# A third tree fetched by row, Silu in place in PSUM, Nyquist sums in two products, and a new order on all engines

## The reference

```python
x = x + attn(layernorm(x));  x = x + ffn(layernorm(x))
# attn: q, k, v = unit_projection(h @ W.T + b)   each frequency divided by its size
#       s = cumsum over the sequence of bind(k, v) = ifft(fft(k) * fft(v))
#       out = unbind(s, q) = ifft(fft(s) * conj(fft(q)))
# ffn:  logits = h @ W_in.T + b_in               8 trees of 255 nodes, depth 7
#       walk each tree from its root, right where the logit is > 0: 8 nodes on the path
#       out = (silu(logits) * on_path) @ W_out.T
```

## Time and profile before

| | |
|---|---|
| median of 3 runs | 1975.06 us (1973.09 to 1975.19) |
| span of the profiled execution, first to last instruction | 1972.4 us |
| the profiled execution's own time | not listed apart; the span is 2.66 us under the median |
| busy: PE, DVE, ACT, POOL | 1883.7, 1579.8, 1118.8, 917.0 us |
| one step in the middle of the loop | 58.56 us |
| start of the first `logits` | 111.50 us |

### The profile page before, as it was taken

How to read it: one execution, slowest core, us unless ns; L and a number is a source line. 1 busy time by engine, 2 the same in 40 slices (tenths; PEclk the granted TensorE clock), 3 DMA queues, 4 the chain that set the end, 5 groups by cost and what they waited for, 6 DMA issues and landing times.

```text
span 1972.4 us, 40210 instructions
## 1 busy us (share of the span) xinstructions
PE 1883.7 (96%) x14680; PEld 1410.5 (72%) x14680; DVE 1579.8 (80%) x2874; ACT 1118.8 (57%) x2151; POOL 917.0 (46%) x736
## 2 busy tenths in 40 slices
PE   8599999999999999999999999999999999999978
PEld 6468777777777777877777877777777777786755
DVE  4887888887888888788888788888788888878783
ACT  5566555566555556555556655556655555655543
POOL 1254444555444555444555444455544455534450
PEclk9799999999999999999999999999999999999998
DMA  8032133222223222223222213222222322222212
GB/s 278 11 86 87 54 96 95 65 85 85 64 85 96 75 80 80 82 67 96 83 77 85 85 53 96 94 66 85 85 64 85 96 75 79 81 71 79 86 54 65
DMA packets 181784, 163.18 MB, mean 83 GB/s; under 512 B 140160, under 2 KB 140800, under 8 KB 181760
## 3 DMA queue, kind: packets, MB, share of 16 engines
q1 hardware_dynamic: 163328, 95.48, 16.2%
q0 software_dynamic: 18432, 67.38, 10.2%
HBM read 95.72 MB, written 16.78 MB: 57 GB/s over the span
## 4 chain that ended last, share of the span: by engine, by line
PE 74%; DVE 10%; ACT 6%; issue 3%; DMA 0%; ACTq 0%; SPq 0%; DVEq 0%
PE bank_l L531 26%; PE bank_p L481 24%; PE bank_l L591 17%; DVE arena L1220 9%; ACT arena L796 3%; ACT arena L705 2%; PE bank_i L481 2%; PE bank_l L541 2%; ACT arena L806 1%; PE bank_i L552 1%; PE bank_i L562 0%; PE bank_i L559 0%; PE bank_i L560 0%; PE bank_i L561 0%; DVE sp_z L1178 0%
## 5 line engine op out<-in xcount | busy, mean ns | idle before, releaser
L591 PE MATMUL bank_l<-wout_mem,arena 128*128 128x512 f16 x2688 | 606.7, 379 | 38.6 <-DVE arena L1220 38.6
L531 PE MATMUL bank_l<-arena,win_mem 128*128 128x256 f16 x5376 | 626.0, 273 | 14.0 <-DMA arena<-xn_pair 14.0
L531 PEld LDWEIGHTS bank_l<-arena,win_mem 128*128 128x128 f16 x5376 | 527.5, 99 | 75.7 <-DMA arena<-xn_pair 14.2
L591 PEld LDWEIGHTS bank_l<-wout_mem,arena 128*128 128x128 f16 x2688 | 255.5, 98 | 365.8 <-DVE arena L1220 84.3
L481 PE MATMUL bank_p<-arena,wf_hi 128*128 128x256 f16 x3072 | 505.9, 273 | 2.7 <-ACT arena L742 2.7
L986 POOL TENSOR_TENSOR arena<-arena 128x512 f32<-128x512 f32 x96 | 121.9, 1270 | 658.5 <-ACT arena L751 658.5
L481 PE MATMUL bank_p<-arena,wf_lo 128*128 128x256 f16 x1536 | 419.1, 273 | 0.0
L1220 DVE SCALAR_TENSOR_TENSOR arena<-arena,s_act 128x512 f16<-128x512 f32 (+1 forms) x256 | 341.5, 1344 | 28.9 <-ACT arena L806 25.6
L481 PEld LDWEIGHTS bank_p<-arena,wf_hi 128*128 128x128 f16 x3072 | 299.7, 98 | 37.6 <-ACT arena L742 3.0
L796 ACT ACTIVATE arena<-bank_l,bias_in,s_logit 128x256 f32<-128x256 f32 x448 | 229.6, 556 | 142.0 <-PE bank_l L541 141.6
L1213 DVE TENSOR_SCALAR dec<-bank_l,thr,off 128x256 bf16<-128x256 f32 x256 | 135.8, 541 | 121.2 <-PE bank_l L531 120.0
(11 more groups left out here) (178 smaller groups left out, 2607.2 us busy)
## 6 DMA issues: line engine op xcount, KB each, us to landing
arena<-in_x SPq DMA_DIRECT2D x32, 512.0 KB, 3.4
arena<-arena SPq DMA_DIRECT2D x32, 512.0 KB, 2.9
out<-arena SPq DMA_DIRECT2D x64, 256.0 KB, 2.1
wout_mem<-in_w_in_t SPq DMA_DIRECT2D x1, 3584.0 KB, 14.6
arena<-in_w_out_t SPq DMA_DIRECT2D x1, 3584.0 KB, 14.6
arena<-xn_pair SPq DMA_TRANSPOSE x128, 2.7
arena<-in_leaf_rows,leaf_row POOLq DMA_INDIRECT x128, 5.6
win_mem<-in_wq SPq DMA_DIRECT2D x1, 1024.0 KB, 8.5
```

The lines of the kernel that those rows point to most:

```text
L531: mm = pe.matmul(bank_l[t % 4][:, c * T:(c + 1) * T], a[:, k, w:w + P], x2t[:, :, b, k, :], start=(c == 0 and k == 0 and m == 0), stop=((t ...
L591: mm = pe.matmul(bank_l[j][:, :], a[:, m, tok], w[:, m, :], start=(m == 0 and a is a_hi and w is wout_hi), stop=(m == DENSE - 1 and a is a ...
```

## The change

- `GATHERED` is (0, 1, 2) for (0, 1): 13 columns for 14, six indirect fetches in a step for four.
- `silu` writes over the logits in PSUM, and `act_high` and `act_low` read them there; the SBUF ring `acts` goes. A bank is free only when `act_low` has read it, so `logits` and `down` wait for `a_lo_ready` where they waited for `act_ready`.
- `nyquist_sums` makes its three columns in two matmuls for five; `nyquist_bind` prepares `sp_kv` with three small instructions for one.
- The order of the groups is K, V, Q for Q, K, V, in the loads, the prologue and every step.
- `unbind` waits after each product until it has been written.
- The prologue: thirty dummy matmuls first, K's weights loaded first, `project(1, ...)` ahead of the first `transform_back`, and all four `wout_high`/`wout_low` in step 0.
- `decide` has four buffers (`HELD`), and every engine's list in `step` is in a new order.

```diff
-GATHERED = (0, 1)
+GATHERED = (0, 1, 2)
-HELD = 3
+HELD = 4
-Q, K, V, G_IN, G_OUT = range(5)
+K, V, Q, G_IN, G_OUT = range(5)
+WARM = 30
...
-        acts = take(HELD * 2 * T).rearrange("p (r t) -> p r t", r=HELD)
...
                 if c == 0 and t >= 4:
 
-                    pe.wait_ge(act_ready, TREES * i + t - 3)
+                    pe.wait_ge(a_lo_ready, TREES * i + t - 3)
...
-                pe.matmul(sp_sums[:, 0:1], upper, sp_kv[:, 0:1], start=True, stop=True)
-                pe.matmul(sp_sums[:, 1:2], upper, sp_kv[:, 1:2], start=True, stop=False)
-                pe.matmul(sp_sums[:, 1:2], full, sp_kv[:, 0:1], start=False, stop=True)
-                pe.matmul(sp_sums[:, 2:3], full, sp_kv[:, 0:1], start=True, stop=False)
-                pe.matmul(sp_sums[:, 2:3], full, sp_kv[:, 1:2], start=False, stop=True).then_inc(sp_sums_full, 1)
+                pe.matmul(sp_sums[:, 0:3], upper, sp_kv[:, 0:3], start=True, stop=False)
+                pe.matmul(sp_sums[:, 0:3], full, sp_kv[:, 2:5], start=False, stop=True).then_inc(sp_sums_full, 1)
...
                 act.wait_ge(count_full, TREES * i + t + 1)
-                if t >= HELD:
-                    act.wait_ge(a_lo_ready, TREES * i + t + 1 - HELD)
-                elif not isinstance(i, int) or i:
-                    act.wait_ge(a_lo_ready, TREES * i)
                 for c in [c for c in range(2) if (t, c) in COLUMN]:
-                    ins = act.activation(acts[:, t % HELD, c * T:(c + 1) * T], bank_l[t % 4][:, c * T:(c + 1) * T],
+                    ins = act.activation(bank_l[t % 4][:, c * T:(c + 1) * T], bank_l[t % 4][:, c * T:(c + 1) * T],
                                          ACT.Silu, bias=bias_in[:, c, t:t + 1], scale=s_logit[:, 0:1])
...
                 dve.scalar_tensor_tensor(out=a_lo[:, m, :],
-                                         in0=acts[:, t % HELD, 0:wide * T].rearrange("p (c t) -> p c t", c=wide),
+                                         in0=bank_l[t % 4][:, 0:wide * T].rearrange("p (c t) -> p c t", c=wide),
                                          scalar=s_act[:, 0:1], in1=a_hi[:, m, :], op0=ALU.mult,
                                          op1=ALU.subtract).then_inc(a_lo_ready, 1)
...
-                pool.tensor_tensor(prod[:, 0], sr, qr, ALU.mult)
-                pool.tensor_tensor(prod[:, 1], si, qi, ALU.mult)
-                pool.tensor_tensor(prod[:, 2], si, qr, ALU.mult)
+                pool.tensor_tensor(prod[:, 0], sr, qr, ALU.mult).then_inc(z_prod, 1)
+                pool.wait_ge(z_prod, 4 * n + 1)
+                pool.tensor_tensor(prod[:, 1], si, qi, ALU.mult).then_inc(z_prod, 1)
+                pool.wait_ge(z_prod, 4 * n + 2)
+                pool.tensor_tensor(prod[:, 2], si, qr, ALU.mult).then_inc(z_prod, 1)
+                pool.wait_ge(z_prod, 4 * n + 3)
                 pool.tensor_tensor(prod[:, 3], sr, qi, ALU.mult).then_inc(z_prod, 1)
...
```

More of the change, by code:

```diff
@@ L266, in build @@
         sp_hat_ready = sem("sp_hat_ready")
+        sp_bound = sem("sp_bound")
         sp_kv_ready = sem("sp_kv_ready")
@@ L864, in first @@
                     fold_high(m)
-                for c in range(PIECES):
-                    win_rows(c)
-                    fold_high(KT + c)
+                projection_rows(Q)
+                for m in range(KT):
+                    fold_high(KT + m)
                 act.wait_ge(consts_done, 1)
+                evac_re(0, K)
+                evac_im(0, K)
+                square(0, K)
+                fold_high(2 * KT)
+                root(0, K)
+                win_rows(0)
+                win_rows(1)
+                evac_re(0, V)
+                evac_im(0, V)
+                square(0, V)
+                fold_high(2 * KT + 1)
+                root(0, V)
+                fold_high(2 * KT + 2)
+                win_rows(2)
+                fold_high(2 * KT + 3)
+                win_rows(3)
+                std(1, mv1, rs1, ln1_mv, ln1_std)
                 evac_re(0, Q)
@@ L1074, in step @@
                     add_eps(n, K)
+                    sum_squares(n, Q)
+                    add_eps(n, Q)
+                    bind(n)
+                for g in range(LEAVES):
+                    fetch(i, g)
+                if attn:
                     q_unit(n)
-                    bind(n)
-                fetch(i, 1)
-                fetch(i, 0)
-                if attn:
                     unbind(n)
```

364 lines of the change are left out of this document (191 added, 173 removed).

## The result

The changed kernel takes 1950.63 us, the median of four runs (1946.7 to 1958.03), against 1974.3 us for the kernel before beside it: a ratio of 0.9891, 95% interval 0.9879 to 0.9904. It is faster, by 1.1%; the forecast was 1895 us and its range 1842 to 1937. Both missed. The profiled execution of after is the slowest of the four, 1958.03 us with a span of 1956.2.

What follows compares the result with a forecast made beforehand. PE's own work bounds the kernel, with a little of DVE. Step: 58.56 - 3.25 - 1.17 + 1.70 + 0.35 = 56.2 us; 30 steps save 71.1, ends 6.2 and 2.6: span 1892.5, plus 2.7, 1895 us; range 1842 to 1937.

Steps and rivals of the forecast that it cites:

- PE's work: Matmuls of one step: fewer logits and `down` columns and Nyquist matmuls save 3.25 us, 57.39 becomes 54.14 us.
- The old wait: PE's wait for `act_low` at `down`: goes with `act_low` from PSUM, 1.17 us less per step.
- the bank's longer hold: PSUM banks of the logits, held until `act_low` has read them: costs nothing.
- The new wait: PE at the first logits, as `evac_im` stands ahead of `high` on ACT: 1.70 us per step.
- The 0.35 us of allowance: End of the step on DVE, dots meeting POOL's unbinding: 0.35 us per step added for what spills over.
- DVE's end: Rival: ten of twelve dots and additions meet POOL, late results bound the step at 57.6 us; 1938 us, chance 0.18.
- The prologue: Before the first logits: transform some 6 us earlier, logits at 102 for 111.50, -9.5 us; bounds 0 and -15.7.
- a hole: PE's idle time from 60 to 80 us: the 15.7 us of `project(1)` move into it.
- Step 0: Four `wout_low` between DVE's decisions make them late, +6.6 us; first full `project` still 6.2 us earlier than 154.87.
- ACT and POOL: Two more table loads, 2.57 us of ACT, cost nothing; POOL ends z at T+52.8, ahead of PE's T+54.6.
- Last block: Block without projection: one column less of logits and of `down`, 2.6 us less.

Runs made afterwards that it cites:

- e10: Changed kernel without the waits between POOL's unbinding products, and with the Nyquist sums in five one-column matmuls again; 1975.31 us.
- b1: Kernel before with only `silu`, `act_high` and `act_low` in PSUM and tree 1's two instructions moved ahead; 2139.75 us, ratio 1.0849.
- e3b: Changed kernel with 18 throwaway matmuls on PE between projections and first logits of steps 1 to 30; 1920.55 us, ratio to before 0.9727.
- e13: The kernel of e3b once more, on another chip beside e14 and e15; 1913.22 us.
- e15: The changed kernel, unchanged, run again as control beside e13 and e14; 1950.83 us.
- e1: Changed kernel with ACT's `evac_im` of the second group behind `high` of the second layer norm, as in the kernel before; 1934.28 us.
- e5: Changed kernel with another order of PE, ACT and DVE in the prologue alone, `project(0, Q)` ahead of W_in's peak among others; 1946.81 us.
- e14: Changed kernel with e3b's 18 throwaway matmuls and e5's prologue order together, run beside e13 and e15; 1905.76 us, ratio to before 0.9677.
- e7: Changed kernel with e5's prologue and, on ACT, `std` and `high` of xn2 ahead of `square(K)` and `evac_im(V)`; 1977.68 us.
- e9: The kernel of e7 with DVE's `decide` of tree 0 ahead of `kv_denominator` and the first inverse; 2039.92 us.
- b4: Kernel before with only `GATHERED = (0, 1, 2)`, its dots, additions and fetches added where the others stand; 2227.61 us, ratio 1.1292.
- e6: Changed kernel with `GATHERED = (0, 1)`, the third tree dense again and the rest of the change kept; 2189.54 us.
- e12: Changed kernel with 9 throwaway matmuls, for e3b's 18, before the first logits; 1943.59 us.
- e8: Changed kernel with e5's prologue, e1's edit and DVE's `decide(i, 0)` ahead of `kv_denominator` and the first inverse; 1977.39 us.

## Why the prediction was wrong

It was right that the kernel gets faster, and in the mechanisms that it wrote down for a step. Two steps of it failed: it left what the granted clock does after the new wait out of the sum, and it had the prologue's path wrong. By its own steps, in the profiled run (span 1956.2 for 1892.5 forecast, 63.7 us too much):

- **PE's work**: 54.14 us forecast, 53.73 measured at full clock. Right to 0.4 us, whose place no run shows; e10 gives the sums their 0.66 us.
- **The old wait**: goes, as forecast. But the bank's longer hold costs nothing only by the new order; b1 shows 4.9 us of waits a step without it. The walk that said so was right, for this order. (It names nine columns of `down(i,0)` ahead of T+44.6; its own list and its 44.6 have eleven.)
- **The new wait**: 1.70 us forecast, 2.12 measured. The place and the releaser were right to 0.02 us (`high` at T+11.83); the way from `high` to the logits was short by 0.45 us. It rested on the last block of before, where the second transpose lands in 2.75 us. In after it takes 3.11 us in the step shown and 3.15 in the last block, so it isn't the place in the step that makes it longer; why it is longer in the changed kernel stays open.

```profile
1924.92 2.75 DMA arena<-xn_pair
1912.38 3.15 DMA arena<-xn_pair
```

- **The 0.35 us of allowance**: nothing spilled over. Work 0.41 less, wait 0.42 more and this 0.35 less make a step at full clock 0.3 us shorter (55.88) than the 56.2 forecast. Over 30 steps the forecast was 10 us too high here. DVE's end, a rival, doesn't bound.
- **Not in the sum at all: the granted clock.** "Step: 58.56 - 3.25 - 1.17 + 1.70 + 0.35 = 56.2 us" counts a microsecond of waiting as a microsecond. Here 2.1 us of idleness cost 2.1 and then another 1.67 in 23 of 30 steps, 38 us in the run. That is the larger of the two failed steps, shown by e3b and by e13 against e15. The prediction read a clock of 0.66 in the prologue and 1.00 in the step, and didn't ask what a new gap would do to it.
- **The prologue**: "the transform some 6 us earlier than its end near 92.0". It ends at 118.0 for 86, 32 us late, and the way from there to the logits takes 18.7 us for 16: 102 became 136.66. The step looked at DVE's list alone (`win_low`). In PE's new list the peaks of W_in stand ahead of `project(0, Q)` and those of W_out ahead of the inverse transform; in ACT's, four `win_high` and four `wout_rows`, 13.1 us from 82.47 to 95.56, stand ahead of the evacuations for which `project(1)` waits. How much of the 34.7 us each part is worth, the runs show only in part. The clock's fall at 20 us is 9, in this run (by after against e1). The orders that e5 undoes are 6.5. The other 19 us are open: in e14, which has neither, `project(1)` still holds PE from 73.93 to 91.63 (below), the transform starts at 96.4, behind three `win_low` on DVE, and the logits at 121.3. The 15.7 us that were to go into a hole stand ahead of the transform, but no run moves them back.

```profile
73.93 17.70 PE bank_p L484 x144
```

- **Step 0**: from the first logits to the first full `project` the walk gives 46.7 us (148.7 less 102), and 46.75 were measured. That is in part luck: PE waits 4.42 us for decisions, not 6.6, and the half clock behind the two waits fills the rest (4.47 us for the first 24 logits, 4.83 for the 24 behind the late decision, against 2.79). So all of the 34.7 us by which the first full `project` is late (183.41 for 148.7) were lost by the first logits.
- **ACT and POOL**: nothing waits for the two table loads or for z at the inverse transform. Right.
- **Last block**: -2.4 us for -2.6.

Together 38 - 10 + 34.7 = 63 of the 63.7 us; the profiled run is also 7 us above the median of its kernel, which is why the medians are only 56 us apart. That size fits the 9 us of the fall at 20 us; no trace shows whether the other three runs had it. With those 9 us the clock is 47 of the 63.7. The range was too narrow: its upper end was the price of DVE's end, and no case had a slower clock or a slower start, although the prologue's bounds were known to be those of a guess.

## What to carry to other kernels

Price a new wait of TensorE twice: its length, and what follows it at half the clock; where the wait can't go, matmuls that compute nothing may be worth more than another order (37.6 us here; of four other orders of ACT and DVE, e1's gained some 15 us and e7's to e9's lost). When a change reorders every engine, follow each engine's list through the prologue and not only the one that was late before. A part that does no harm in the full change may cost 8 or 13% alone (b1, b4), so its worth can't be read from an experiment with one part. And compare two prologues by traces in which the clock fell at the same places.

## What the runs showed of the hardware

- **The clock.** At the first logits, PE's gap of 2.1 to 2.2 us is followed by 0.50 for 3.4 us, with PE busy, in 22 of 29 steps of after, 20 of e15, 24 of e10, and in none of e6, which has the same gap there but a longer one of 3.08 us later in the step, with the fall at that one. Gaps of 0.94 and 0.65 us with 2.8 us of work between (e1), of 1.17 us (e12) and of 0.20 us (e13) brought no fall in any step. The length of a gap alone doesn't decide: 1.97 us for a decision (e8) had a fall in 2 of 29 steps, 1.2 and 1.8 us with 2.7 us of work between (e7) in 3, and 2.48 us (b1) in 11. Why one step in three or four with the 2.1 us gap is spared isn't settled.
- **The clock in the prologue.** With the same prologue the clock was at half from about 21 us on for 10 to 14 us, PE busy, in the traces of after, e3b, e13 and e15, and not in those of e1, e10 and e12; the first full `project` starts at 180 to 183 us in the first four and at 174 to 175 in the others.
- **DVE and POOL.** Two scans of 128x256 take 1.39 us in after and 4.10 beside POOL's products (e6), and dots 1370 ns for 680. `act_low` of 128x512 with one input in PSUM takes 740 ns in the mean of the 83 that overlap a tensor instruction of POOL and 738 in the 22 that don't (after, 300 to 1532 us); with both in SBUF it took 2538 ns in the 63 that overlap and 747 in the 63 that don't (before; the 1642 of the earlier trace rows is their mean). The Trainium skill, "SBUF — State Buffer", section "SBUF: two separate sides", states a lock that a DVE instruction with two SBUF inputs and a GpSimd one that reads SBUF take in turn; the 740, the 1370 and the 2538 ns agree with it, and the scans, which read two inputs from SBUF, take three times as long beside two products of POOL.
- **Chips or loads.** The same build took 1944.77 us on one chip and 1905.76 on another, each beside its own runs of before, which agreed to 1.1 us (1973.52 and 1972.43). With one load on each, chip and load can't be told apart. A stable kernel before doesn't show that a changed one is stable.
